# State-space layer of a vision tower: first token as the scan's initial value, product one pair ahead, sums one chunk behind

## The chip, the cores and the metric

One core of a Trainium2 chip. The metric is the device time of one execution in microseconds (us); the kernel is timed in several executions and the median is taken.

## What is computed

A batch of 8 images of 256 x 256 runs through a class-token tower of eight layers on a residual stream of 257 tokens by 256 features: a wavelet tokenizer, memory attention, a mixture of experts, latent attention, a second mixture, **a bidirectional state-space layer**, adapters, a differential attention and a switch layer. The change is in the state-space layer alone. For each of two directions (the second reads the tokens backwards) it computes, with 512 inner features d and 32 states n:

```
u, z   = split(x @ Win.T)
uc     = silu(causal_conv4(u))
dt     = softplus(uc @ Wx_rank @ Wdt + bdt);   B, C = uc @ Wx (32 states each)
h[t,d,n] = exp(dt[t,d] * A[d,n]) * h[t-1,d,n] + dt[t,d] * uc[t,d] * B[t,n],   h before the first token = 0
y[t,d] = sum over n of h[t,d,n] * C[t,n]  + uc * D,  then times silu(z), then @ Wout, a layer norm, and @ Wfuse
```

## The kernel before

Features lie on the 128 partitions and the 257 tokens (T) along the free dimension. The layer is `section_mamba` (L1202). A **unit** is one image in one direction: 16 units, first the 8 forward ones. `units` (L1243) runs them on each engine by a `body` that has the same order of work in each engine's own queue; `before` and `after` say whether a unit has a neighbour whose work is woven into it. The weaving is written by hand as places (n, m).

Within a unit the 512 features are 4 blocks j of 128, and the 32 states are 4 groups q of 8. A **chunk** n = 4j+q (0 to 15, `NCH`) is 8 states of one block, worked as 4 **pairs** m = 0..3 of two states; p = 4n+m numbers the 64 pairs (`SUB`). I call (n, m) a slot. Per pair:

- TensorE, `spread_b` (L1408): two bf16 matmuls that lay one row of B each over all partitions, into a PSUM buffer `pb`. There are 4 rows of `pb`, so two pair buffers; pair p waits for the scans of pair p-2 (semaphore `b_free`).
- VectorE: a product in place (L1740), `pb` times dt*u, for 514 elements, then two scans (L1746) of 257 elements with decays `da` and initial value 0.0, into `hs`. The scans wait for the decays (`da_done`), for the product just before them (`b_set`), and in even m for GpSimd's products of two chunks ago (`hc_done`), since `hs`, `da` and `hc` each have two chunk buffers.
- ScalarE, `decay` (L1617): two exponentials. It works one chunk ahead of VectorE: `decay(n+1, m)` waits until pair (n-1, m) is scanned.
- GpSimd: `hc` = `hs` * C (L1344), four states at a time, two halves per chunk; half 0 waits for scan (n,1) and for the sums of chunk n-2 (`y_free`), half 1 for scan (n,3).
- TensorE, `total` (L1416): adds up the states by fp32 matmuls with the identity, 8 per chunk. In slot (n, m) it issues `spread_b(n, m)` and then `total(n-2, m)`, two chunks behind; in the first two chunks of a unit these are the last two of the unit before.

In chunks 0 to 3 TensorE also spreads the C rows (`spread_c`, L1403, two per slot, behind the sum), ScalarE copies them to SBUF (`cb`, L1648), one pair of copies behind each decay pair, and GpSimd's chunk n waits for its copies (`c_free`).

The next unit's head and the last unit's tail lie in between. On TensorE: projections (L1385) in chunks 4, 5, 7, 8, `b_c_rank` in 9, time steps in 10 to 12; `outward` (L1435) of the unit before in chunk 6, behind a wait for the fourth `take_u` (`proj_free`), then mean, variance, fuse. On ScalarE: `take_u` (L1549, convolution taps of one block, lines L1554 and L1555) behind the decays in chunks 4 to 6, `take_z` (L1557: four silus, a silu of 1028 elements, a table load back) behind chunk 7's, rank, time steps, `soften` and `stack` in 9 to 13; `take_out`, `square`, `root`, `affine` ahead of the decays in 7, 10, 11, 12. On GpSimd: `soften` (L1318, six instructions) behind hc in chunks 0, 2, 12, 14, `taps` (L1304, three of 514 elements) in 5 and 6, small work in 1, 3, 9, 10. On VectorE: `out_chunk` (L1707, two instructions) at (2,0), (6,0), (10,0), (14,0), `center` (L1716) at (9,3), `scale` (L1720) at (11,2), `add` (L1727 or L1729) at (13,2).

`pb` takes four of the eight PSUM banks, `py` (sums) two, `pm` (everything else) two.

Of the kernel before, what the change touches and what calls it, by code (L numbers as in the profile page):

```python
# [17 lines left out]
BF16 = mybir.dt.bfloat16  # L18
# [1183 lines left out]
def section_mamba(nc, k, con, dirs, bfuse):  # L1202
# [6 lines left out]
    with ExitStack() as ctx:  # L1209
# [15 lines left out]
        da = sb("da", [P, 2, NQ_, T])  # L1225
# [43 lines left out]
        with nc.Block() as block:  # L1269
# [19 lines left out]
            def _(pool):  # L1289
# [41 lines left out]
                def body(u, v, d, before, after):  # L1331
                    scanned, summed, c_free = Turn(u, SUB, 2), Turn(u, NCH, 2), Turn(u, NS_, 2)
# [43 lines left out]
            def _(pe):  # L1376
# [31 lines left out]
                def spread_b(u, v, n, m):  # L1408

                    pe.wait_ge(s["b_free"], Turn(u, SUB, 2)(4 * n + m - 1))  # L1410
                    for o in range(2):
                        st = (n % QN) * NQ_ + 2 * m + o
                        ins = nc.tensor.matmul(pb[:, 2 * (m % 2) + o, 0:T], sel[:, st, :], bst2[:, v, :], start=True, stop=True)  # L1413
                    ins.then_inc(s["b_done"], 1)
# [43 lines left out]
                def body(u, v, d, before, after):  # L1458
                    if before is not None:
                        pe.wait_ge(s["f_out"], u + 1)  # L1460
                    pe.wait_ge(s["stacked"], u + 1)
                    pe.wait_ge(s["dt_free"], Turn(u, DJ)(DJ))
                    for n in range(NCH):
                        for m in range(4):
                            spread_b(u, v, n, m)
                            if n >= 2:
                                total(u, n - 2, m)
                            elif before is not None:
                                total(u - 1, NCH - 2 + n, m)
# [3 lines left out]
                            if after is not None:  # L1473
# [64 lines left out]
            def _(act):  # L1538
# [78 lines left out]
                def decay(u, v, d, n, m, free):  # L1617
# [1072 lines left out]
```

## Time and profile before

| what | value |
|---|---|
| time, median of 3 runs | 4842.3 us (4804.22 to 4862.68) |
| the profiled execution | 4836.52 us, its span 4834.8 us |
| TensorE, VectorE, ScalarE, GpSimd busy | 3729.3, 2845.8, 2055.7, 1813.0 us |
| mean granted TensorE clock | 0.895 of 2.4 GHz |

The span runs from the first to the last instruction. Busy time is the union of an engine's instructions, and neighbours overlap a little: an instruction's recorded end lies later than the start of the next, so what an instruction costs its engine is read from start to start in the timeline. The state-space layer lies from about 1571 to 3780 us.

### The profile page before, as it was taken

To read this page: it belongs to the slowest core of one execution; us is meant where nothing else is said; L and a number is where in the kernel's file an instruction comes from. 1 tells how busy PE (TensorE), PEld (TensorE's weight loads), DVE (VectorE), ACT (ScalarE), POOL (GpSimd) and SP (SyncE) were. 2 spreads that over 40 slices of the span, in tenths; PEclk is the share of its full clock that TensorE was granted. 3 is DMA by queue.
4 is the path that set the end of the run, shared out by engine and by line. 5 is a ranking of instruction groups with operands and counts; after the bars stand their busy time and mean duration, and the time that the engine had idled before them with its cause. 6 is when DMAs were issued, how large, how long until landed. Compare 5 with 4: busy or idle time off the path is not lost. (4 is left out here: it accounts for less than half of the span.)

```text
span 4834.8 us, 61153 instructions
## 1 busy us (share of the span) xinstructions
PE 3729.3 (77%) x19350; PEld 2506.0 (52%) x19350; DVE 2845.8 (59%) x4980; ACT 2055.7 (43%) x4651; POOL 1813.0 (37%) x1405
## 2 busy tenths in 40 slices
PE   2848758987986777777778887777776778888857
PEld 1525445655653455555555555555554655555534
DVE  5311224443222999899999999898999433333331
ACT  1211112223113666666666656666665233333322
POOL 0120110000102777777777777777776000000011
PEclk9679959998998899989999999898999999999965
DMA  2157520001472000000000000000000000000035
GB/s 80 45 185 264 210 56 1 1 1 48 163 272 90 1 1 1 2 1 2 1 11 1 1 7 1 2 1 2 1 1 1 9 22 1 1 1 1 1 117 167
DMA packets 94875, 214.46 MB, mean 44 GB/s; under 512 B 13792, under 2 KB 69088, under 8 KB 84224
## 3 DMA queue, kind: packets, MB, share of 16 engines
q1 hardware_dynamic: 71136, 177.89, 10.8%
q0 software_dynamic: 6400, 16.85, 1.1%
q10 hardware_dynamic: 16992, 15.47, 0.9%
q8 instruction: 172, 2.82, 0.2%
q14 instruction: 175, 1.43, 0.1%
HBM read 166.61 MB, written 43.56 MB: 43 GB/s over the span
## 5 line engine op out<-in xcount | busy, mean ns | idle before, releaser
L1344 POOL TENSOR_TENSOR ssm_hc<-ssm_hs,ssm_cb 128x1028 f32<-128x1028 f32 x512 | 1204.5, 2367 | 525.0 <-PE ssm_py L1425 411.9
L1746 DVE TENSOR_TENSOR_SCAN ssm_hs<-ssm_da,ssm_pb 128x257 f32<-128x257 f32 x2048 | 1299.1, 677 | 125.5 <-ACT ssm_da L1625 4.5
L1425 PE MATMUL ssm_py<-ssm_hc,ident 128*128 128x257 f32 x4096 | 1155.2, 407 | 3.5 <-issue 3.5
L1625 ACT ACTIVATE ssm_da<-ssm_dt,ssm_an 128x256 f32<-128x256 f32 x2048 | 878.4, 505 | 155.4 <-DVE ssm_hs L1746 149.6
L1425 PEld LDWEIGHTS ssm_py<-ssm_hc,ident 128*128 128x128 f32 x4096 | 760.5, 207 | 97.2 <-issue 4.1
L1740 DVE TENSOR_TENSOR ssm_pb<-ssm_pb,ssm_dtu 128x514 f32<-128x514 f32 x1024 | 695.0, 679 | 96.6 <-PE ssm_pb L1413 59.2
L1413 PE MATMUL ssm_pb<-ssm_bst,ssm_sel 96*128 96x257 bf16 x2048 | 430.5, 294 | 410.4 <-DVE ssm_hs L1746 400.1
L1413 PEld LDWEIGHTS ssm_pb<-ssm_bst,ssm_sel 96*128 96x128 bf16 x2048 | 143.1, 101 | 732.9 <-DVE ssm_hs L1746 678.7
L1095 DVE TENSOR_REDUCE duo_mxr<-duo_ring 128x4 f32<-128x1024 f32 x128 | 156.6, 1225 | 315.0 <-PE duo_ring L828 303.9
L2182 PE MATMUL moe_pu<-moe_up,moe_xt 128*128 128x512 f32 x568 | 277.4, 612 | 54.4 <-issue 52.5
L1648 ACT COPY ssm_cb<-ln_ps 128x257 f32<-128x257 f32 x512 | 166.1, 377 | 218.7 <-PE ln_ps L1406 217.8
L2079 POOL DMA_INDIRECT moe_yg<-moe_y_dram,moe_slot x51 | 48.2, 945 | 554.5 <-DMA moe_y_dram<-moe_yo 539.5
L2458 DVE COPY moe_ht<-moe_pz 128x512 f32<-128x512 f32 x71 | 49.1, 692 | 298.8 <-PE moe_pz L2192 298.8
L822 PE MATMUL duo_ring<-duo_k,duo_q 32*128 32x256 f32 x1024 | 146.2, 403 | 45.3 <-DVE duo_mxr L1095 45.0
L2182 PEld LDWEIGHTS moe_pu<-moe_up,moe_xt 128*128 128x128 f32 x568 | 100.5, 194 | 145.0 <-issue 140.8
L986 ACT ACTIVATE duo_ex<-duo_ring 128x1024 f32<-128x1024 f32 x128 | 130.9, 1024 | 102.5 <-PE duo_ring L828 102.5
L728 POOL TENSOR_TENSOR duo_qb<-duo_bm,duo_q 128x4 f32<-128x4 f32 x32 | 6.3, 197 | 425.3 <-ACT duo_k L970 425.3
L728 POOL TENSOR_TENSOR lat_qb<-lat_bm,lat_q 128x4 f32<-128x4 f32 x32 | 6.4, 200 | 421.6 <-DVE lat_k L1083 421.6
L822 PEld LDWEIGHTS duo_ring<-duo_k,duo_q 32*128 32x128 f32 x1024 | 93.4, 187 | 101.3 <-issue 47.5
L828 PE MATMUL duo_ring<-duo_q,duo_k 32*128 32x256 f32 x1024 | 145.9, 404 | 0.0
L1385 PE MATMUL ln_ps<-xb,ssm_win 128*128 128x257 f32 x512 | 135.4, 388 | 12.1 <-ACT ssm_e L1555 6.5
L282 PE MATMUL ln_ps<-h,mean 128*128 128x257 f32 x160 | 55.8, 481 | 112.0 <-PEq L80 62.0
(528 smaller groups left out, 5941.1 us busy)
## 6 DMA issues: line engine op xcount, KB each, us to landing
moe_up<-in_moe_up SPq DMA_DIRECT2D x72, 1024.0 KB, 5.0
moe_down<-in_moe_down SPq DMA_DIRECT2D x72, 512.0 KB, 5.8
moe_xr<-moe_x_dram SPq DMA_DIRECT2D x71, 128.0 KB, 5.7
moe_y_dram<-moe_yo ACTq DMA_DIRECT2D x71, 128.0 KB, 1.7
sw_wt<-in_sw_w SPq DMA_DIRECT2D x47, 192.5 KB, 2.5
sw_x_dram<-sw_zero SPq DMA_DIRECT2D x1, 6016.0 KB, 19.4
sw_xr<-sw_x_dram SPq DMA_DIRECT2D x47, 128.0 KB, 2.4
sw_y_dram<-sw_yo ACTq DMA_DIRECT2D x47, 128.0 KB, 1.7
```

The lines of the kernel that those rows point to most:

```text
L822: ins1 = nc.tensor.matmul(dst1[:, o, at:at + w], q[r, b1, t * P:t * P + P], kk[r, b1, a, 0:w], start=not causal, stop=not causal or t == 1)
L828: ins2 = nc.tensor.matmul(dst2[:, o, at:at + 256 - q0], kk[r, b2, a, t * P:t * P + P], q[r, b2, q0:256], start=not causal, stop=not causal ...
L1095: ins = nc.vector.tensor_reduce(mxr[:, a, js, :], src.rearrange("p o (t s) -> p o t s", t=2), AX, ALU.max)
L1344: nc.gpsimd.tensor_tensor(hc[:, n % 2, part_], hs[:, n % 2, part_], cb[:, q * NQ_ + 4 * half:q * NQ_ + 4 * half + 4, :], ALU.mult).then_in ...
L1385: ins = nc.tensor.matmul(pm[:, n % 2, 0:T], w_in[:, c, n * P:n * P + P], k.xb[:, c, 0:T], start=(c == 0), stop=(c == C - 1))
L1413: ins = nc.tensor.matmul(pb[:, 2 * (m % 2) + o, 0:T], sel[:, st, :], bst2[:, v, :], start=True, stop=True)
L1425: ins = nc.tensor.matmul(py[:, j % 2, 0:T], k.ident[:], hc[:, n % 2, st, :], start=(q == 0 and st == 0), stop=(q == QN - 1 and st == NQ_ - 1))
L1625: ins = nc.scalar.activation(da[:, n % 2, 2 * m + o, 1:T], dt2[:, v, j, 1:T], ACT.Exp, scale=a_n[:, d, j, st:st + 1])
L1648: nc.scalar.copy(cb[:, st, :], pm[:, st % 2, 0:T]).then_inc(s["c_free"], 1)
L1740: nc.vector.tensor_tensor(b2, b2, dtu2[:, v, j:j + 1, :].broadcast_to([P, 2, T]), ALU.mult).then_inc(s["b_set"], 1)
L1746: ins = nc.vector.tensor_tensor_scan(hs[:, n % 2, 2 * m + o, :], da[:, n % 2, 2 * m + o, :], b2[:, o, :], 0.0, ALU.mult, ALU.add)
L2182: ins = nc.tensor.matmul(pu[:, b % 2, g, :], xt[:, b % 2, c, :], up[:, b % WR, c, g * HID:g * HID + HID], start=(c == 0), stop=(c == C - 1))
```

## The change

- `pb` becomes four pair buffers of 2 x 256 elements (a pair in one bank); token 0 is taken out of it. B's first token comes by its own small matmul (`first_b`), ScalarE copies it to `b0` (`take_first`), and once per chunk ScalarE writes dt*u*B of token 0 for the chunk's 8 states into `hs[..., 0]` (`start`). Scans take that as initial value and run over tokens 1 to 256.
- VectorE issues the product of pair p+1 ahead of the scans of pair p; TensorE spreads B two pairs ahead of the slot and may do so when the scans of four pairs ago are done.
- TensorE sums chunk n-1 in chunk n.
- The fourth `take_u` moves ahead of the decays in chunk 6.

Core of the diff (semaphore names, the memset of `da` that goes, and the copy of the identity to bf16 for `first_b` left out):

```diff
-        da = sb("da", [P, 2, NQ_, T])
+        eyeb = sb("eyeb", [3 * NS_, NS_], BF16)
+        b0 = sb("b0", [P, 2, NS_])
+        da = sb("da", [P, 2, NQ_, T - 1])
-        pb = ps("pb", [P, 4, BANK])
+        pb = ps("pb", [P, 4, 2, T - 1])
...
+                def first_b(u, v):
+                    pe.wait_ge(s["stacked"], u + 1)
+                    nc.tensor.matmul(pm[:, 0, 0:NS_], bst2[:, v, 0:1].broadcast_to([3 * NS_, P]), eyeb[:], start=True, stop=True).then_inc(s["first_done"], 1)
-                def spread_b(u, v, n, m):
-                    pe.wait_ge(s["b_free"], Turn(u, SUB, 2)(4 * n + m - 1))
+                def spread_b(u, v, p):
+                    pe.wait_ge(s["b_free"], Turn(u, SUB, 4)(p - 3))
                     for o in range(2):
-                        ins = nc.tensor.matmul(pb[:, 2 * (m % 2) + o, 0:T], sel[:, st, :], bst2[:, v, :], start=True, stop=True)
+                        ins = nc.tensor.matmul(pb[:, p % 4, o, :], sel[:, st, :], bst2[:, v, 1:T], start=True, stop=True)
...
-                    pe.wait_ge(s["stacked"], u + 1)
+                    pe.wait_ge(s["first_out"], u + 1)
                     for n in range(NCH):
                         for m in range(4):
-                            spread_b(u, v, n, m)
-                            if n >= 2:
-                                total(u, n - 2, m)
+                            if 4 * n + m + 2 < SUB:
+                                spread_b(u, v, 4 * n + m + 2)
+                            elif after is not None:
+                                spread_b(u + 1, 1 - v, 4 * n + m + 2 - SUB)
+                            if n:
+                                total(u, n - 1, m)
                             elif before is not None:
-                                total(u - 1, NCH - 2 + n, m)
+                                total(u - 1, NCH - 1, m)
...
+                                if (n, m) == (14, 2):
+                                    if before is not None:
+                                        pe.wait_ge(s["f_out"], u + 2)
+                                    first_b(u + 1, 1 - v)
...
+                def take_first(u, v):
+                    act.wait_ge(s["first_done"], u + 1)
+                    nc.scalar.copy(b0[:, v, :], pm[:, 0, 0:NS_]).then_inc(s["first_out"], 1)
+
+                def start(u, v, n, free):
+                    j, q = n // QN, n % QN
+                    if n == 0:
+                        act.wait_ge(s["first_out"], u + 1)
+                    if free is not None:
+                        act.wait_ge(s["hc_done"], free)
+                    nc.scalar.activation(hs[:, n % 2, :, 0], b0[:, v, q * NQ_:q * NQ_ + NQ_], ACT.Copy, scale=dtu2[:, v, j, 0:1]).then_inc(s["h_first"], 1)
...
                     for n in range(NCH):
+                        if n == 6 and after is not None:
+                            take_u(u + 1, 1 - v, after, 3)
...
+                        free = Turn(u, 2 * NCH, 4)(2 * n) if n or before is not None else None
+                        if n + 1 < NCH:
+                            start(u, v, n + 1, free)
+                        elif after is not None:
+                            start(u + 1, 1 - v, 0, free)
...
-                            if n == 6:
-                                take_u(u + 1, 1 - v, after, 3)
...
+                            if n == 14:
+                                take_first(u + 1, 1 - v)
...
+                def product(u, v, p):
+                    j = p // (4 * QN)
+                    if p % (4 * QN) == 0:
+                        dve.wait_ge(s["dt_set"], Turn(u, DJ)(j + 1))
+                    b2 = pb[:, p % 4]
+                    dve.wait_ge(s["b_done"], Turn(u, SUB)(p + 1))
+                    nc.vector.tensor_tensor(b2, b2, dtu2[:, v, j:j + 1, 1:T].broadcast_to([P, 2, T - 1]), ALU.mult).then_inc(s["b_set"], 1)
...
                         for m in range(4):
-                            b2 = pb[:, 2 * (m % 2):2 * (m % 2) + 2, 0:T]
-                            dve.wait_ge(s["b_done"], Turn(u, SUB)(4 * n + m + 1))
-                            nc.vector.tensor_tensor(b2, b2, dtu2[:, v, j:j + 1, :].broadcast_to([P, 2, T]), ALU.mult).then_inc(s["b_set"], 1)
+                            p = 4 * n + m
+                            if p + 1 < SUB:
+                                product(u, v, p + 1)
+                            elif after is not None:
+                                product(u + 1, 1 - v, 0)
                             if m % 2 == 0:
                                 dve.wait_ge(s["hc_done"], Turn(u, 2 * NCH, 4)(2 * n + m // 2 - 3))
+                            if m == 0:
+                                dve.wait_ge(s["h_first"], Turn(u, NCH)(n + 1))
+                            dve.wait_ge(s["da_done"], Turn(u, SUB)(p + 1))
+                            dve.wait_ge(s["b_set"], Turn(u, SUB)(p + 1))
                             for o in range(2):
-                                ins = nc.vector.tensor_tensor_scan(hs[:, n % 2, 2 * m + o, :], da[:, n % 2, 2 * m + o, :], b2[:, o, :], 0.0, ALU.mult, ALU.add)
+                                st = 2 * m + o
+                                ins = nc.vector.tensor_tensor_scan(hs[:, n % 2, st, 1:T], da[:, n % 2, st, :], pb[:, p % 4, o, :], hs[:, n % 2, st, 0:1], ALU.mult, ALU.add)
```

## Rows read from the trace of the kernel before

**Rows 1.** Stretches view: length; busy PE, PEld, DVE, ACT, POOL; clock. Layer, one unit.

```profile
1577.00:3760.00 2183.00, 1714.03 (x7835) 1182.42 (x7836) 1989.23 (x3254) 1355.77 (x3288) 1620.38 (x1067) 0.92 0.01 2
...
2582.00:2718.60 136.60, 108.58 (x497) 75.16 (x497) 124.61 (x205) 86.27 (x209) 102.49 (x69) 0.92 0.00 1
```

**Rows 2.** The page's list of costliest groups, three of the layer.

```profile
L1344 POOL TENSOR_TENSOR ssm_hc<-ssm_hs,ssm_cb 128x1028 f32<-128x1028 f32 x512 | 1204.5, 2367 | 525.0 <-PE ssm_py L1425 411.9
L1746 DVE TENSOR_TENSOR_SCAN ssm_hs<-ssm_da,ssm_pb 128x257 f32<-128x257 f32 x2048 | 1299.1, 677 | 125.5 <-ACT ssm_da L1625 4.5
...
L1740 DVE TENSOR_TENSOR ssm_pb<-ssm_pb,ssm_dtu 128x514 f32<-128x514 f32 x1024 | 695.0, 679 | 96.6 <-PE ssm_pb L1413 59.2
```

**Rows 3.** Timeline of VectorE: start, duration, line, idle before it.

```profile
2614.37 0.68 DVE L1740 TENSOR_TENSOR ssm_pb<-ssm_pb,ssm_dtu 128x514 f32<-128x514 f32 x1
2615.15 1.27 DVE L1746 TENSOR_TENSOR_SCAN ssm_hs<-ssm_da,ssm_pb 128x257 f32<-128x257 f32 x2
2616.33 0.67 DVE L1716 TENSOR_TENSOR ln_cen<-ln_sq,ln_ps 128x514 f32<-128x514 f32 x1
2616.91 0.70 DVE L1740 TENSOR_TENSOR ssm_pb<-ssm_pb,ssm_dtu 128x514 f32<-128x514 f32 x1
...
2618.92 0.47 DVE L1710 SCALAR_TENSOR_TENSOR ssm_py<-ssm_uc,ssm_cols,ssm_py 128x257 f32<-128x257 f32 x1
2619.42 0.42 DVE L1712 TENSOR_TENSOR ssm_zs<-ssm_zs,ssm_py 128x257 f32<-128x257 f32 x1
2619.76 0.69 DVE L1740 TENSOR_TENSOR ssm_pb<-ssm_pb,ssm_dtu 128x514 f32<-128x514 f32 x1
...
2648.08 0.85 DVE L1727 SCALAR_TENSOR_TENSOR h<-ln_ps,ssm_lnc,h 128x257 f32<-128x257 f32 x2
2648.85 0.69 DVE L1740 TENSOR_TENSOR ssm_pb<-ssm_pb,ssm_dtu 128x514 f32<-128x514 f32 x1
```

**Rows 4.** Who waited for whom over the execution: us, times, longest.

```profile
DVE ssm_pb L1740 <- PE ssm_pb L1413: 59.2, 40, 2.6
```

**Rows 5.** Timeline of TensorE and VectorE in chunk 6 of a unit.

```profile
2718.50 2.08 PE L1435 MATMUL ln_ps<-ssm_zs,ssm_wout 128*128 128x257 f32 x4 [3.18 <-ACT ssm_e L1555]
...
2721.05 0.70 DVE L1740 TENSOR_TENSOR ssm_pb<-ssm_pb,ssm_dtu 128x514 f32<-128x514 f32 x1 [2.25 <-PE ssm_pb L1413]
```

**Rows 6.** Timeline of ScalarE: two copies of C rows; silu, table load, decays.

```profile
2667.18 0.65 ACT L1648 COPY ssm_cb<-ln_ps 128x257 f32<-128x257 f32 x2 [4.56 <-PE ln_ps L1406]
...
2739.30 1.05 ACT L1562 ACTIVATE ssm_uc<-ssm_e 128x1028 f32<-128x1028 f32 x1
2740.37 1.28 ACT L1563 ACT_TABLE_LOAD   x1
2741.67 3.70 ACT L1625 ACTIVATE ssm_da<-ssm_dt,ssm_an 128x256 f32<-128x256 f32 x9
```

**Rows 7.** Timeline of TensorE at the high and at the low clock.

```profile
2665.79 0.38 PE L1413 MATMUL ssm_pb<-ssm_bst,ssm_sel 96*128 96x257 bf16 x2 [0.82 <-DVE ssm_hs L1746]
2666.01 1.03 PE L1425 MATMUL ssm_py<-ssm_hc,ident 128*128 128x257 f32 x4
2666.88 0.38 PE L1406 MATMUL ln_ps<-ssm_cst,ssm_sel 96*128 96x257 bf16 x2
...
2690.64 1.92 PE L1425 MATMUL ssm_py<-ssm_hc,ident 128*128 128x257 f32 x4
2692.35 0.64 PE L1406 MATMUL ln_ps<-ssm_cst,ssm_sel 96*128 96x257 bf16 x2
```

**Rows 8.** Timeline of GpSimd: soften begins, hc behind it; taps, hc behind them.

```profile
2678.41 0.72 POOL L1323 TENSOR_TENSOR ssm_e<-ssm_e,ssm_dtu 128x257 f32<-128x257 f32 x1
...
2683.38 4.69 POOL L1344 TENSOR_TENSOR ssm_hc<-ssm_hs,ssm_cb 128x1028 f32<-128x1028 f32 x2
...
2732.45 1.28 POOL L1310 TENSOR_TENSOR ssm_e<-ssm_e 128x514 f32<-128x514 f32 x1
...
2736.50 2.36 POOL L1344 TENSOR_TENSOR ssm_hc<-ssm_hs,ssm_cb 128x1028 f32<-128x1028 f32 x1
```

More of the change, by code:

```diff
@@ L1331, in body @@
                 def body(u, v, d, before, after):
-                    scanned, summed, c_free = Turn(u, SUB, 2), Turn(u, NCH, 2), Turn(u, NS_, 2)
+                    scanned, summed, c_free = Turn(u, SUB, 4), Turn(u, NCH, 2), Turn(u, NS_, 2)
                     for n in range(NCH):
@@ L1523, in _ @@
                     time_step(0, j)
+                first_b(0, 0)
+                for p in range(2):
+                    spread_b(0, 0, p)
                 units(pe, body)
                 last = UN - 1
-                for n in (NCH - 2, NCH - 1):
-                    for m in range(4):
-                        total(last, n, m)
+                for m in range(4):
+                    total(last, NCH - 1, m)
                 pe.wait_ge(s["f_out"], last + 2)
@@ L1638, in body @@
                         for m in range(4):
-                            free = Turn(u, SUB, 2)(4 * (n - 1) + m + 1) if n or before is not None else None
+                            free = Turn(u, SUB, 4)(4 * (n - 1) + m + 1) if n or before is not None else None
                             if n + 1 < NCH:
@@ L1681, in _ @@
                 stack(0, 0)
+                take_first(0, 0)
                 for m in range(4):
                     decay(0, 0, 0, 0, m, None)
+                start(0, 0, 0, None)
                 units(act, body)
@@ L1695, in _ @@
                 link = Link(dve, k.dve_link)
-                link(nc.vector.memset(da[:, :, :, 0:1], 0.0))
                 dve.wait_ge(s["w_in"], 16 * 13)
                 nc.vector.tensor_scalar_min(a_n[:], a_n[:], 83.0).then_inc(s["rates"], 1)
+                nc.vector.tensor_copy(eyeb[:], eye3[:])
                 nc.vector.tensor_copy(sel[:], eye3[:].unsqueeze(2).broadcast_to([3 * NS_, NS_, P])).then_inc(s["sel_set"], 1)
-                dve.sem_inc(s["b_free"], 2)
+                dve.sem_inc(s["b_free"], 4)
                 dve.sem_inc(s["y_free"], 2)
@@ L1733, in body @@
                     for n in range(NCH):
-                        j, q = n // QN, n % QN
-                        if q == 0:
-                            dve.wait_ge(s["dt_set"], Turn(u, DJ)(j + 1))
+                        q = n % QN
+                        j = n // QN
                         for m in range(4):
-                            b2 = pb[:, 2 * (m % 2):2 * (m % 2) + 2, 0:T]
-                            dve.wait_ge(s["b_done"], Turn(u, SUB)(4 * n + m + 1))
-                            nc.vector.tensor_tensor(b2, b2, dtu2[:, v, j:j + 1, :].broadcast_to([P, 2, T]), ALU.mult).then_inc(s["b_set"], 1)
+                            p = 4 * n + m
[3 more added lines that the diff above has]
+                                product(u + 1, 1 - v, 0)
@@ L1741, in body @@
                             if m % 2 == 0:
                                 dve.wait_ge(s["hc_done"], Turn(u, 2 * NCH, 4)(2 * n + m // 2 - 3))
-                            dve.wait_ge(s["da_done"], Turn(u, SUB)(4 * n + m + 1))
-                            dve.wait_ge(s["b_set"], Turn(u, SUB)(4 * n + m + 1))
+                            if m == 0:
+                                dve.wait_ge(s["h_first"], Turn(u, NCH)(n + 1))
+                            dve.wait_ge(s["da_done"], Turn(u, SUB)(p + 1))
@@ L1758, in body @@
                                     add(u - 1, before)
+                product(0, 0, 0)
                 units(dve, body)
```

6 lines of the change are left out of this document (3 added, 3 removed).

## The prediction

> **What bounds the kernel now.** The change lies in one of nine stages, the state-space layer, so I first cut that stage out with the stretches view. From 1577 to 3760 us VectorE is busy 1989 of 2183 us, GpSimd 1620, TensorE 1714 and ScalarE 1356 [rows 1]: VectorE sets the pace. The layer is sixteen units (8 images, two directions); one of them is the stretch of 136.6 us. A unit has 64 slots (n,m), n = 0..15, m = 0..3, and a slot on VectorE is a product (L1740) and two scans (L1746). I call the end of the last scan of chunk n F(n).
>
> The cost list gives what VectorE spends on the two [rows 2]: 1299 us in 2048 scans with 125.5 us idle in front of them, which the view gives almost nobody as releaser, and 695 us in 1024 products. 125.5/1024 = 0.12 us a slot is the scan's wait for the product just before it (semaphore b_set). The timeline shows it better, from start to start [rows 3]: a product holds VectorE 0.78 us when its own scan follows (2614.37 to 2615.15; 0.80 in even slots), but an instruction of the same 514 elements holds it 0.58 when the follower depends on nothing recent (L1716 at 2616.33, product at 2616.91). Two scans take 1.18. So a slot is 1.97 to 1.99, 64 make 126.7, and the rest of VectorE's unit is four pairs L1710/L1712 at 0.84, L1716 and L1720 at 0.58, and 0.77 for the two of L1727: 5.3. With some 4 us of true waiting this is 136.6.
>
> That waiting is TensorE's late B rows: 59.2 us in 40 waits [rows 4]. It sits in chunk 6: TensorE waits 3.18 us for the last convolution copy of ScalarE (L1555) before it may start L1435, and VectorE then lacks the input of a product for 2.25 us [rows 5] and that of the next for somewhat less.
>
> **The parts of the change, with prices.**
> *Product one pair ahead, four pair buffers.* Between product p+1 and its scan there now lie two scans, so the product costs 0.58 and not 0.79: -0.21 us a slot. One token fewer (256 for 257, 512 for 514) is worth under 0.01. This asks that B rows come two slots earlier, which the buffers permit: TensorE may write pair p once scan p-4 is done.
>
> The 0.78 with a wait and the 0.58 without stand in the timeline [rows 3]. The Trainium skill speaks against this term: its page "VectorE: DVE Perf Modes", section "The DRAIN you can't avoid", says that the next VectorE op does not start until the pipe has emptied and that a semaphore between two ops "costs nothing extra here". By that rule the term would be 0; the trace does not agree, and I go by the trace.
>
> *First token as initial value.* 2048 scans read their start from memory and not from the instruction. No scan here does. The nearest rows: L1712 (two tensors, 257 elements) holds VectorE 0.34 us (2619.42 to 2619.76), L1727, which also reads a per-partition value, (2648.85-2648.08)/2 = 0.385 [rows 3]. Bounds 0 and 0.045 us a scan (0 to 92 us in all); I take 0.045, the only row of that kind. A slot becomes 0.58+1.18+0.09 = 1.86 (bounds 1.77 and 1.86). Four slots: 7.44. VectorE's unit: 64 x 1.86 + 5.3 = 124.3.
>
> *take_u of the fourth block ahead of the decays of chunk 7.* It no longer waits for scan (5,3), so the wait of chunk 6 goes. I give it 52 of the 59.2 us (the rest is start-up and single late rows), 3.7 us in each of the 14 units that have both neighbours.
>
> *ScalarE's new work*: 16 starts of 128x8 and one copy per unit, 0.2 to 0.3 us each by my estimate (two copies of 257 elements take 0.65 in [rows 6]): 4 to 5 us in a unit where ScalarE has 50 free. The work costs nothing, but its place does: start(n+1) stands behind all four decays and, in chunks 0 to 3, behind the eight copies of C of chunk n, and scan (n+1,0) waits for it. Before, that scan needed the first decay only. It also waits for GpSimd's products of chunk n-1, both halves.
>
> *Sums one chunk behind.* GpSimd's 412 us of waits for TensorE [rows 2] go, and TensorE gets a wait instead: in slot (n,0) it waits for half 0 of hc(n-1), in (n,2) for half 1, and behind it in its queue stand C rows, projections and the B rows of the next slots. I follow that through a unit. Durations: B or C pair 0.22, total pair 0.87, another fp32 pair 0.87 [rows 7]; two halves of hc 4.7, one 2.35, soften 4.97, taps 4.05 [rows 8]; the last of two copies ends 0.95 behind its C pair (2666.88 to 2667.83), more when a decay runs; silu of 1028 elements 1.05, table load 1.28, a decay 0.41 [rows 6].
>
> Clock from F(14)=0, F(15)=7.4. GpSimd: hc(14) to 2.4, soften to 7.4, hc(15) to 9.8 and 12.1. TensorE (0,0) is held to 9.8, then a slot costs 0.87+0.22+0.22 = 1.31; C rows 6, 7 go out at 14.6, copied 15.65, start(1) 15.9; VectorE wants it at 15.5: late 0.45, and 0.35 by product 7. hc(0) begins at 15.65 (it needs those copies), half 0 to 18.0; the same again: start(2) at 24.2, wanted 23.4: 0.8. hc(0) ends 20.4, soften 25.3, half 0 of hc(1) 27.7; TensorE is held to that, B rows for product 11 come 0.9 late, start(3) 0.4 late. Chunk 3: 0.65. hc(2) runs from 33.6 to 38.3, soften to 43.2, half 0 of hc(3) to 45.6; TensorE (4,0) then does total, projection and the B rows: ready 47.7, wanted 45.1: 2.55. Together 6.1 us.
>
> Clock from F(5)=0 (F(6)=8.3, F(7)=15.7, F(8)=23.4): hc(5) to 2.45, taps to 6.5, hc(6) to 11.2, taps to 15.25, half 0 of hc(7) to 17.6. TensorE (8,0): total, projection, B rows, total, projection to 21.3. ScalarE: silu 21.8, silu 1028 22.9, table load 24.15, four decays 27.4, start(9) 27.7. VectorE wants it at 24.0: 3.7 late; with 0.2 for product 35, 3.9. In chunks 9 to 15 I find every answer in time, by 1.3 us or more.
>
> *Sum.* Unit: 136.6 - 64x0.12 (7.7) - 3.7 + 6.1 + 3.9 = 135.2; walking VectorE's own clock round (124.3 + 9.8, where late answers overlap and the small old waits fall away) gives 134.1. I take the walk: -2.5 x 14 = -35. First and last unit have half of the stalls: -6. A start-up copy and wait: +1. TensorE's clock: in the unit the mean grant is 0.92 [rows 1], that is 0.08/0.5 or 0.16 of the time (22 us) at 1.2 GHz and not 2.4, and a total pair then costs 1.71 instead of 0.87 [rows 7]. Until now such stretches had cover; where TensorE is held by GpSimd it has none. I put 1 us a unit on it, +14. Sum -26. The profiled execution took 4836.5 us (span 4834.8), 6 below the median of the runs, 4842.3: 4836.5-26 = 4810.
>
> **The rivals.**
> 1. *The new waits are hidden* (against the walk; for it: GpSimd is busy 102 of 136 us and could be earlier than I think). Then -7.7-3.7 in 14 units, -7.7 in two: -175, 4661. With a free initial value another -92: 4570.
> 2. *The initial value costs nothing.* Only 30 to 35 slots of a unit are not tied to the GpSimd-TensorE loop, so -2.8 us a unit, not -5.8: 4765.
> 3. *Slower: a loop takes over.* Place: chunks 0 to 4 and 8. C rows wait behind the sum, the sum for GpSimd, GpSimd for the copies of the C rows. With TensorE at 1.2 GHz a slot is near 2.6 and the loop 2.35+4x2.6 = 12.7 against 7.44. If half of the 22 us a unit falls there, half of those 11 us is lost: 5 us, unit 139.2 and not 134.1, 4836.5+14x2.6 = 4873. It decides from 2.5 us of added waits a unit. For it: TensorE will stand still 2 to 3 us at (8,0), and before the low stretch of chunk 6 it stood still 3.18 us [rows 5].
> 4. *No overlap of product and scan.* A product still holds VectorE 0.79 with other scans behind it: slot 1.97+0.09 = 2.06, +5.8 a unit, -3.7, and some 5 of the 10 us of stalls (they shrink when VectorE is slower): +7 x 15 = +105, 4940. Against it are the 0.58 us [rows 3]; this is also the case in which the change does not do what it says. (It is what the Trainium skill's section named above would have.)
>
> **How the numbers follow.** Forecast 0.47; rival 1 0.17 (in part or in full); rival 2 0.15; rival 3 0.18; rival 4 0.03. The measurement tells about 2% from no change, so faster means under 4745, slower over 4939. Faster: rival 1 (0.15), half of rival 2 (0.06), the low tail of the forecast (0.06): 0.27. Slower: rival 4 (0.02), the upper end of rival 3 (0.06), others 0.02: 0.10. Range: up to rival 3 with its spread, 4895, down to the price of rival 1, 4665. The forecast's own range is 4765 to 4860.
>
> **What the profile after would show.** Product to next scan start 0.58 and no 0.12 us in front of each scan. Scans of 0.72 us if the initial value costs, 0.67 if not. No wait of L1435 for L1555 in chunk 6. GpSimd's wait for TensorE's sums nearly gone; in its place TensorE waits for hc, above all in slots (4,0), (7,0) and (8,0). Scans with a wait for ScalarE's start in chunks 1 to 4, and one of 3 to 4 us at (9,0). Unit near 134 us. The prediction is wrong if TensorE's waits for hc are there and VectorE has none, or if VectorE waits over 12 us a unit.

## The result and the profile after

The changed kernel takes 4919.6 us (median of 4 runs, 4918.3 to 4948.6) against 4839.6 (4804.2 to 4862.7): a ratio of 1.0186, interval 1.0113 to 1.0259 (here and in the table below the ratio is the record's estimate over all runs, not the quotient of the two medians). I had forecast 4810 with a range of 4665 to 4895. The profiled execution took 4919.25 us, its span is 4917.5.

The stretches view of the changed kernel: the layer, then two stretches of 5 us.

```profile
1577.00:3850.00 2273.00, 1758.28 (x7833) 1258.55 (x7834) 2017.88 (x3243) 1403.65 (x3571) 1619.11 (x1072) 0.89 0.01 2
2720.00:2725.00 5.00, 1.39 (x3) 1.17 (x4) 4.98 (x8) 0.00 (x0) 4.92 (x4) 0.82 0.00 0
2725.00:2730.00 5.00, 5.00 (x17) 3.54 (x16) 2.82 (x5) 2.90 (x8) 0.87 (x1) 0.50 0.02 3
```

The layer answers to [rows 1]: 90 us longer, TensorE's granted clock 0.89 and not 0.92, and VectorE idle for 255 us of it where it was idle for 194. From the first scan to the end of the last the layer now lasts 2276 us (before: 2184). That length is my measure below, since what lies outside the layer differs by up to 61 us from one profiled execution to another (2608 us in e5, 2669 in f3), in parts of the program that no kernel here alters.

The cost list of the changed kernel, four of the layer's largest groups (L1797 is the scan, L1777 the product, L1346 GpSimd's hc, L1432 the sum):

```profile
L1432 PE MATMUL ssm_py<-ssm_hc,ident 128*128 128x257 f32 x4096 | 1230.1, 427 | 385.0 <-POOL ssm_hc L1346 384.8
L1797 DVE TENSOR_TENSOR_SCAN ssm_hs<-ssm_da,ssm_hs,ssm_pb 128x256 f32<-128x256 f32 x2048 | 1410.5, 731 | 103.0 <-ACT ssm_hs L1655 93.0
L1346 POOL TENSOR_TENSOR ssm_hc<-ssm_hs,ssm_cb 128x1028 f32<-128x1028 f32 x512 | 1204.0, 2363 | 619.2 <-DVE ssm_hs L1797 410.6
...
L1777 DVE TENSOR_TENSOR ssm_pb<-ssm_pb,ssm_dtu 128x512 f32<-128x512 f32 x1024 | 697.6, 681 | 178.9 <-PE ssm_pb L1420 144.1
```

Held against [rows 2]: GpSimd no longer waits for TensorE's sums (411.9 us before). TensorE instead stands 385 us in front of its sums, waiting for GpSimd. VectorE's 0.12 us in front of every scan is gone; the 103 us there now are the late start (L1655), and its products wait 144 us for B rows, where they waited 59.2 [rows 4]. A scan, recorded, has grown from 677 to 731 ns.

VectorE's timeline away from the stalls, which answers to [rows 3]:

```profile
2603.98 0.68 DVE L1777 TENSOR_TENSOR ssm_pb<-ssm_pb,ssm_dtu 128x512 f32<-128x512 f32 x1
2604.57 1.38 DVE L1797 TENSOR_TENSOR_SCAN ssm_hs<-ssm_da,ssm_hs,ssm_pb 128x256 f32<-128x256 f32 x2
2605.86 0.68 DVE L1777 TENSOR_TENSOR ssm_pb<-ssm_pb,ssm_dtu 128x512 f32<-128x512 f32 x1
```

A product holds VectorE 0.59 us from start to start, two scans 1.29: a slot of 1.875 us. I forecast 1.86.

I took the start of every scan pair out of VectorE's timeline and subtracted the undisturbed slot and the known insertions (L1748 and the like) from each distance; what is left over is lost waiting. Mean of the 14 units with both neighbours:

| | slot | unit | lost a unit | where |
|---|---|---|---|---|
| before | 1.985 | 137.2 | 4.9 | chunk 6: 3.7 |
| after | 1.875 | 143.3 | 18.0 | chunks 0 to 4: 3.2, 2.6, 1.9, 2.7, 2.3 (12.7); around (9,0): 5.1 |

A wait in front of the first scan of chunk n+1 is counted to chunk n here. So the places are those of the prediction but for chunk 0, to which the walk gave 0.45 us and not 3.2, and the wait of chunk 6 is gone. The size is not the predicted one: 18 us where the walk had 10. What a stall looks like, in the timeline of TensorE (first chunk of a unit, and the first sum of chunk 2):

```profile
2717.77 1.03 PE L1432 MATMUL ssm_py<-ssm_hc,ident 128*128 128x257 f32 x4
...
2723.61 2.08 PE L1432 MATMUL ssm_py<-ssm_hc,ident 128*128 128x257 f32 x4 [3.73 <-POOL ssm_hc L1346]
2725.49 0.64 PE L1408 MATMUL ln_ps<-ssm_cst,ssm_sel 96*128 96x257 bf16 x2
2725.92 0.63 PE L1420 MATMUL ssm_pb<-ssm_bst,ssm_sel 96*128 96x256 bf16 x2
2726.34 1.92 PE L1432 MATMUL ssm_py<-ssm_hc,ident 128*128 128x257 f32 x4
...
2735.12 1.14 PE L1432 MATMUL ssm_py<-ssm_hc,ident 128*128 128x257 f32 x4 [2.87 <-POOL ssm_hc L1346]
...
2744.71 2.08 PE L1432 MATMUL ssm_py<-ssm_hc,ident 128*128 128x257 f32 x4 [4.07 <-POOL ssm_hc L1346]
```

and of VectorE and GpSimd in the same chunks:

```profile
2726.59 0.70 DVE L1777 TENSOR_TENSOR ssm_pb<-ssm_pb,ssm_dtu 128x512 f32<-128x512 f32 x1 [1.61 <-PE ssm_pb L1420]
...
2732.70 4.68 POOL L1346 TENSOR_TENSOR ssm_hc<-ssm_hs,ssm_cb 128x1028 f32<-128x1028 f32 x2 [6.83 <-ACT ssm_cb L1679]
```

TensorE stands 3.73 us for GpSimd, and the sum behind it takes 2.08 us where the one before took 1.03. In the 5 us from 2725 the granted clock is 0.50, the lower of its two levels (1.2 GHz). A slot of TensorE then lasts 2.7 us (2723.61 to 2726.34), 1.3 at the upper level (2736.09 to 2737.41). The C rows come out later by that, ScalarE's copies behind them, GpSimd's hc of this chunk behind those (6.83 us of waiting), and that sets the next sum. Behind 4.07 us the same happens; behind 2.87 the sum takes 1.14 and the clock holds.

Around chunk 8 a stand of 2.33 us precedes slower projections (L1387: 1.58 us, then 1.15, where 1.03 is usual), the silus wait for them, and the start of chunk 9 comes 3.44 us late:

```profile
2653.61 1.14 PE L1432 MATMUL ssm_py<-ssm_hc,ident 128*128 128x257 f32 x4 [2.33 <-POOL ssm_hc L1346]
2654.59 1.58 PE L1387 MATMUL ln_ps<-xb,ssm_win 128*128 128x257 f32 x4
...
2665.52 1.39 DVE L1797 TENSOR_TENSOR_SCAN ssm_hs<-ssm_da,ssm_hs,ssm_pb 128x256 f32<-128x256 f32 x2 [3.44 <-ACT ssm_hs L1655]
```

### The profile page after: what moved, and what is told of

Same layout as the page of the kernel before. It is cut to its first block and busy times, and to the rows that moved or that the text cites. A ratio compares the mean times of both kernels' runs of the same rounds, so it can differ in the third digit from the quotient of the medians.

```text
span 4917.5 us, 61727 instructions
## 1 busy us (share of the span) xinstructions
PE 3749.6 (76%) x19366; PEld 2567.9 (52%) x19366; DVE 2881.8 (59%) x4980; ACT 2098.2 (43%) x4923; POOL 1812.7 (37%) x1405
## 5 line engine op out<-in xcount | busy, mean ns | idle before, releaser
L1432 PE MATMUL ssm_py<-ssm_hc,ident 128*128 128x257 f32 x4096 | 1230.1, 427 | 385.0 <-POOL ssm_hc L1346 384.8
L1797 DVE TENSOR_TENSOR_SCAN ssm_hs<-ssm_da,ssm_hs,ssm_pb 128x256 f32<-128x256 f32 x2048 | 1410.5, 731 | 103.0 <-ACT ssm_hs L1655 93.0
L1346 POOL TENSOR_TENSOR ssm_hc<-ssm_hs,ssm_cb 128x1028 f32<-128x1028 f32 x512 | 1204.0, 2363 | 619.2 <-DVE ssm_hs L1797 410.6
L1432 PEld LDWEIGHTS ssm_py<-ssm_hc,ident 128*128 128x128 f32 x4096 | 788.8, 214 | 551.4 <-POOL ssm_hc L1346 431.6
L1777 DVE TENSOR_TENSOR ssm_pb<-ssm_pb,ssm_dtu 128x512 f32<-128x512 f32 x1024 | 697.6, 681 | 178.9 <-PE ssm_pb L1420 144.1
L1420 PE MATMUL ssm_pb<-ssm_bst,ssm_sel 96*128 96x256 bf16 x2048 | 433.1, 296 | 119.6 <-DVE ssm_hs L1797 115.0
L1420 PEld LDWEIGHTS ssm_pb<-ssm_bst,ssm_sel 96*128 96x128 bf16 x2048 | 190.2, 105 | 333.7 <-DVE ssm_hs L1797 219.5
L1387 PE MATMUL ln_ps<-xb,ssm_win 128*128 128x257 f32 x512 | 149.2, 419 | 8.2 <-DVE ssm_sel L1738 4.8
```

Source lines behind the costliest of these rows:

```text
L1346: nc.gpsimd.tensor_tensor(hc[:, n % 2, part_], hs[:, n % 2, part_], cb[:, q * NQ_ + 4 * half:q * NQ_ + 4 * half + 4, :], ALU.mult).then_in ...
L1387: ins = nc.tensor.matmul(pm[:, n % 2, 0:T], w_in[:, c, n * P:n * P + P], k.xb[:, c, 0:T], start=(c == 0), stop=(c == C - 1))
L1420: ins = nc.tensor.matmul(pb[:, p % 4, o, :], sel[:, st, :], bst2[:, v, 1:T], start=True, stop=True)
L1432: ins = nc.tensor.matmul(py[:, j % 2, 0:T], k.ident[:], hc[:, n % 2, st, :], start=(q == 0 and st == 0), stop=(q == QN - 1 and st == NQ_ - 1))
L1777: nc.vector.tensor_tensor(b2, b2, dtu2[:, v, j:j + 1, 1:T].broadcast_to([P, 2, T - 1]), ALU.mult).then_inc(s["b_set"], 1)
L1797: ins = nc.vector.tensor_tensor_scan(hs[:, n % 2, st, 1:T], da[:, n % 2, st, :], pb[:, p % 4, o, :], hs[:, n % 2, st, 0:1], ALU.mult, ALU.add)
```

## The experiments

"Layer" is from the first scan to the end of the last in the profiled execution; slot, unit and lost are the tally above. Ratios are to the kernel before, run on the same chip.

| run | median us | ratio (interval) | layer | slot | unit | lost |
|---|---|---|---|---|---|---|
| before | 4839.6 | | 2184 | 1.985 | 137.2 | 4.9 |
| after | 4919.6 | 1.0186 (1.0113 to 1.0259) | 2276 | 1.875 | 143.3 | 18.0 |
| e1 sums two behind | 4664.4 | 0.9623 (0.9583 to 0.9662) | 2024 | 1.875 | 126.8 | 1.5 |
| e2 C rows first | 4909.2 | 1.0144 (1.0100 to 1.0188) | 2264 | 1.875 | 142.8 | 17.5 |
| e3 start early | 4917.9 | 1.0142 (1.0094 to 1.0189) | 2273 | 1.875 | 143.1 | 17.8 |
| e4 zero initial value | 4863.5 | 1.0032 (1.0005 to 1.0058) | 2221 | 1.755 | 139.8 | 22.2 |
| e5 keep the clock | 4859.0 | 1.0064 (1.0030 to 1.0099) | 2214 | 1.875 | 139.2 | 13.9 |
| e6 take_u alone | 4759.7 | 0.9853 (0.9786 to 0.9919) | 2132 | 1.985 | 133.5 | 1.2 |
| e7 two behind, start early | 4813.0 | 0.9948 (0.9913 to 0.9983) | 2153 | 1.875 | 135.3 | 10.0 |
| e8 product between scans | 4665.5 | 0.9643 (0.9555 to 0.9731) | 2032 | 1.78 | 127.5 | 8.3 |
| f1 one behind alone | 5093.5 | 1.0553 (1.0530 to 1.0576) | 2434 | 1.985 | 153.5 | 21.1 |
| f2 two behind, take_u back | 4758.1 | 0.9830 (0.9778 to 0.9881) | 2122 | 1.875 | 133.9 | 8.6 |
| f3 two behind, own slot | 4902.9 | 1.0157 (1.0129 to 1.0185) | 2237 | 2.09 | 140.1 | 1.0 |

The experiments ran on three chips: the kernel before had a median of 4839.6 us beside e1 to e4, 4838.1 beside e5 to e8 and 4829.2 beside f1 to f3. Where runs of different chips are compared below, the difference of their medians can be off by some 10 us, and the layer's length is the better measure.

**e1. The changed kernel with the sums two chunks behind again.**

```diff
-                            if n:
-                                total(u, n - 1, m)
+                            if n >= 2:
+                                total(u, n - 2, m)
                             elif before is not None:
-                                total(u - 1, NCH - 1, m)
+                                total(u - 1, NCH - 2 + n, m)
```

> The changed kernel with one part undone: TensorE sums chunk n-2 in chunk n again; everything else of the change stays. Theory A (the loop: with sums one chunk behind TensorE waits for GpSimd's hc, and the B and C rows queued behind the sum come late, at a clock that the standing still has lowered): the unit falls from 143.3 us by most of the 12.5 us that VectorE loses in chunks 0 to 4 and by about 3 in chunk 8, to 128 to 131 us; time 4710 to 4760; TensorE's wait for hc (385 us) gone, GpSimd's wait for TensorE's sums back (some 200 to 400 us) and harmless. Theory B (the place of ScalarE's start behind the decays and copies is the price, 93 us of waits): 4830 to 4919. Theory C (the initial value read from memory is the price, 0.055 us a scan): unchanged, 4919.

4664 us, 255 below the changed kernel and 175 below the kernel before, and 46 below what theory A allowed at best; theories B and C are out as the main cause. The cost list of e1 from 1577 us on:

```profile
L1798 DVE TENSOR_TENSOR_SCAN ssm_hs<-ssm_da,ssm_hs,ssm_pb 128x256 f32<-128x256 f32 x2039 | 1401.4, 729 | 14.7 <-ACT ssm_hs L1656 11.8 <-POOL ssm_hc L1346 2.6 <-issue 0.3
L1346 POOL TENSOR_TENSOR ssm_hc<-ssm_hs,ssm_cb 128x1028 f32<-128x1028 f32 x511 | 1200.8, 2367 | 365.7 <-PE ssm_py L1432 300.7 <-ACT ssm_cb L1680 36.8 <-DVE ssm_hs L1798 22.5
L1432 PE MATMUL ssm_py<-ssm_hc,ident 128*128 128x257 f32 x4096 | 1092.4, 390 | 1.2 <-POOL ssm_hc L1346 1.2
...
L1778 DVE TENSOR_TENSOR ssm_pb<-ssm_pb,ssm_dtu 128x512 f32<-128x512 f32 x1018 | 686.8, 675 | 2.0 <-issue 1.2 <-PE ssm_pb L1420 0.5
```

TensorE's 385 us of waiting for hc are 1.2, and everything that VectorE waited for goes with them. GpSimd waits 301 us for TensorE again, which costs nothing here: 1.5 us a unit are lost. The sums' place makes 16.5 of the 18.0 us a unit. Putting it back also makes the wait for the start nearly vanish (93 to 12 us), though the start's own place is unchanged.

**f1. The other side: the kernel before, with the sums one chunk behind and nothing else** (the same edit the other way round).

> The kernel before with one edit: TensorE sums chunk n-1 in chunk n. No initial value, no product ahead, no moved convolution, no start. Theory (the place of the sums is what costs, whoever waits behind it): the wait of TensorE for GpSimd's products of chunk n-1 stands ahead of the B rows of the next slot, and here B rows are only one slot ahead of VectorE, not two. The sum's place cost 18.0 - 1.5 = 16.5 us a unit in the changed kernel; I expect 12 to 18 here, about +230 us: 5070 (4980 to 5130), with VectorE's products waiting for TensorE's B rows for over 150 us. Rival (the price belongs to the pair of one-behind sums and the late start of the initial value, which the kernel before has not): only the C-row loop is left, 2 to 4 us a unit, 4870 to 4900.

5093.5, 264 above the kernel before, near the theory's 5070. VectorE's products wait for B rows:

```profile
DVE ssm_pb L1739 <- PE ssm_pb L1413: 291.3, 208, 3.5
```

The edit costs 250 us of layer in this kernel, which has no start of an initial value, and 252 in the changed one, which has it. The rival is out, and the other parts hide none of it.

**e2 and e3. Which wait, if not the sums' place?** e2 issues the C rows of a slot ahead of its sum; e3 issues the start behind the second pair of decays and not behind the fourth and the copies.

```diff
+                            if n < QN:
+                                spread_c(u, v, NQ_ * n + 2 * m)
+                                spread_c(u, v, NQ_ * n + 2 * m + 1)
                             if n:
                                 total(u, n - 1, m)
...
                             if n < QN:
-                                spread_c(u, v, NQ_ * n + 2 * m)
-                                spread_c(u, v, NQ_ * n + 2 * m + 1)
```

> The changed kernel, but in chunks 0 to 3 TensorE issues the two C rows of a slot ahead of the sum and not behind it. A: cuts the link sum -> C rows -> copies -> hc and start, so chunks 0 to 3 lose 6 to 8 us less a unit and hc(3) is earlier for slot (4,0); B rows of chunk 4 and 8 stay late: 4810 to 4850. B: start(n+1) no longer waits for late copies in chunks 1 to 4, but for the rest: 4860. C: 4919.

> The changed kernel, but ScalarE's start of the next chunk stands behind the second decay pair and not behind all four and their copies. A: only the wait at (9,0) shrinks (1.6 of 3.4 us), chunks 1 to 4 stay tied to late B rows: 4880 to 4905. B: the 93 us of waits for start go nearly all: 4830. C: 4919.

Neither moves the time: their medians lie 10 and 2 us below the changed kernel's, and the runs of all three overlap. The numbers of A and B both missed, and C's 4919 was met without C being right: its cause, the initial value, is not the price (e1, e4). What moved is the name of the wait. Who waited for whom, first e2, then e3 (us in total, times, longest):

```profile
DVE ssm_pb L1777 <- PE ssm_pb L1420: 180.1, 137, 4.5
...
DVE ssm_hs L1797 <- ACT ssm_hs L1655: 58.0, 36, 3.4
```

```profile
DVE ssm_pb L1778 <- PE ssm_pb L1420: 208.6, 146, 4.7
...
DVE ssm_hs L1798 <- ACT ssm_hs L1655: 28.7, 16, 2.3
```

The wait for the start falls from 93 to 58 and 29, the one for B rows rises from 144 to 180 and 209. I read both as answers of one late loop, where the sooner of them only uncovers the other. Something else moved too: over the four executions of each the mean granted clock is 0.873 in e2 and 0.876 in e3, in the changed kernel 0.885. So some of what the edits gave may have gone into a lower clock; no run separates the two.

**e4. Initial value 0.0 in every scan** (the contribution of each unit's first token is left out; everything else, the start too, is still issued).

```diff
-ins = nc.vector.tensor_tensor_scan(hs[:, n % 2, st, 1:T], da[:, n % 2, st, :], pb[:, p % 4, o, :], hs[:, n % 2, st, 0:1], ALU.mult, ALU.add)
+ins = nc.vector.tensor_tensor_scan(hs[:, n % 2, st, 1:T], da[:, n % 2, st, :], pb[:, p % 4, o, :], 0.0, ALU.mult, ALU.add)
```

> The changed kernel, but the scans take the constant 0.0 as initial value (the first token's contribution is left out of the states; start still writes it). The scan should return from 0.645 to 0.59 us start to start, the slot from 1.875 to 1.765. C: all 2048 x 0.055 = 113 us come back: 4806. A: only the slots that are not tied to the loop (30 to 40 of 64) give anything: 45 to 65 us, 4855 to 4875, and the other slots show the same wait longer.

```profile
L1797 DVE TENSOR_TENSOR_SCAN ssm_hs<-ssm_da,ssm_pb 128x256 f32<-128x256 f32 x2048 | 1284.0, 668 | 104.1 <-ACT ssm_hs L1655 91.4 <-issue 12.8
```

A scan takes 668 ns, not 731, and the slot is 1.755, 0.01 less than expected: the initial value costs 0.06 us a scan from start to start (0.053 net against the scans of 257 elements before: two took 1.186 us, now 1.293). Of the 7.7 us a unit that this frees (64 x 0.12) the unit gets 3.5, and the waits grow from 18.0 to 22.2. More than half of the gain is lost to the loop, as A said.

**e5. Eight matmuls that nobody reads, ahead of the sums in six slots of a unit**, to keep TensorE at work where it would stand.

```diff
+                            if (n, m) in ((0, 0), (1, 0), (2, 0), (3, 0), (4, 0), (8, 0)) and (n or before is not None):
+                                pe.wait_ge(s["b_free"], Turn(u, SUB, 4)(4 * n))
+                                for _ in range(8):
+                                    nc.tensor.matmul(pb[:, (4 * n + 3) % 4, 0, 0:P], k.ident[:], k.ident[:], start=True, stop=True)
                             if n:
                                 total(u, n - 1, m)
```

> The changed kernel with eight added matmuls of the identity (128 columns, result overwritten by the next B rows) in slots (0,0), (1,0), (2,0), (3,0), (4,0), (8,0), where TensorE otherwise stands still for GpSimd's hc. They do no useful work; they wait for what the next B rows wait for. Theory K (a good part of the stalls is TensorE at 1.2 GHz just behind each standing still): VectorE's loss in chunks 0 to 4 falls from 12.7 us a unit to 7 to 9, granted clock in the layer up from 0.89 to 0.94 or more, time 4830 to 4870. Theory L (the order of the waits alone makes the loss): no gain, the added work costs 0 to 1 us a unit, 4919 to 4935.

4859 us, 61 below the changed kernel; the layer is 62 shorter. TensorE's timeline at two such places and at one without added matmuls:

```profile
2683.61 2.05 PE L1479 MATMUL ssm_pb<-ident 128*128 128x128 f32 x16
2687.70 1.14 PE L1432 MATMUL ssm_py<-ssm_hc,ident 128*128 128x257 f32 x4 [2.04 <-POOL ssm_hc L1346]
...
2701.68 2.05 PE L1479 MATMUL ssm_pb<-ident 128*128 128x128 f32 x16
2705.77 1.42 PE L1432 MATMUL ssm_py<-ssm_hc,ident 128*128 128x257 f32 x4 [2.03 <-POOL ssm_hc L1346]
...
2790.14 2.08 PE L1432 MATMUL ssm_py<-ssm_hc,ident 128*128 128x257 f32 x4 [3.82 <-POOL ssm_hc L1346]
```

and the stretches view of chunks 0 to 4 of one unit, in the changed kernel, e5 and e1:

```profile
2721.70:2772.60 50.90, 36.30 (x162) 27.31 (x163) 39.64 (x64) 29.99 (x86) 35.07 (x28) 0.83 0.00 1
2667.70:2713.70 46.00, 39.85 (x240) 32.20 (x239) 39.28 (x63) 29.81 (x87) 35.07 (x28) 0.96 0.00 1
2582.00:2620.50 38.50, 30.51 (x161) 20.90 (x160) 38.47 (x64) 28.35 (x80) 36.14 (x29) 1.00 0.01 1
```

Work that computes nothing, put into a queue that is too late already, makes the kernel faster: chunks 0 to 4 lose 8.3 us a unit, not 12.7, chunk 8 loses 4.3, not 5.1, and the layer's granted clock is 0.93, not 0.90 (theory K had 0.94 or more). The added matmuls can only delay TensorE's queue, so the gain is the clock's. In the 14 middle units, chunks 0 to 4 have 19.2 us a unit at the lower level in the changed kernel and 3.9 in e5. They do not hold the clock everywhere: at 2705.77 it falls even so, and the last row of TensorE's timeline shows a place without them. So the clock is a part of the loss, at least 4 us a unit; 13.9 are left, and e5 loses 1.2 of them in chunk 11, where the changed kernel loses nothing.

**e6. The kernel before with the fourth take_u ahead of the decays of chunk 6, alone.**

```diff
+                        if n == 6 and after is not None:
+                            take_u(u + 1, 1 - v, after, 3)
                         if n == 7 and before is not None:
...
-                            if n == 6:
-                                take_u(u + 1, 1 - v, after, 3)
```

> The kernel before with one part of the change alone: the fourth take_u ahead of the decays of chunk 6. If its price is what the prediction says, the 3.7 us that VectorE loses in chunk 6 go in 14 units: 4785 to 4795. If another wait takes its place (the decays of chunk 7 come 1.5 us later), 4820 to 4840.

```profile
L1740 DVE TENSOR_TENSOR ssm_pb<-ssm_pb,ssm_dtu 128x514 f32<-128x514 f32 x1022 | 693.5, 679 | 16.5 <-PE ssm_pb L1413 10.4 <-issue 6.0
```

The unit is 3.7 us shorter, the layer 52, which is the predicted price to the digit. The stand of 3.18 us in chunk 6 [rows 5] goes with it, and the layer's granted clock is 0.96 where it was 0.92. The median falls by 78, more than expected; the other 26 lie outside the layer of the profiled execution, and no part of the edit reaches there. The interval (down 0.8 to 2.1%) holds both numbers.

**f2. e1 with that take_u back in its old place.**

> The changed kernel with sums two chunks behind, as in e1, and the fourth take_u back behind the decays of chunk 6. Theory (its price is the late B rows of chunk 6, as alone): +3.7 us in 14 units, 4664 + 52 = 4716, up to 4664 + 78 = 4742 if it is worth what it was alone. Rival (with four pair buffers TensorE is a slot further ahead and covers half of it): +1.8 a unit, 4690.

94 us above e1 (on another chip; the layer is 98 longer), more than either theory had. TensorE and VectorE in chunk 6 of f2:

```profile
2672.99 2.08 PE L1442 MATMUL ln_ps<-ssm_zs,ssm_wout 128*128 128x257 f32 x4 [5.67 <-ACT ssm_e L1572]
...
2675.53 0.70 DVE L1778 TENSOR_TENSOR ssm_pb<-ssm_pb,ssm_dtu 128x512 f32<-128x512 f32 x1 [4.03 <-PE ssm_pb L1420]
```

In [rows 5] these are 3.18 and 2.25. The same wait is longer, I take it because VectorE now gets to chunk 6 sooner and ScalarE's convolution does not; 5.9 us a unit are lost in chunk 6 and 2.3 in chunk 8. TensorE's stand reaches VectorE less 1.64 us (5.67 to 4.03), where it was 0.93 (3.18 to 2.25): the extra buffers cover far from half, so the rival is wrong, and so is the theory's price, which took the wait as a constant.

**f3. e1 with product p in its own slot.**

```diff
-                            if p + 1 < SUB:
-                                product(u, v, p + 1)
-                            elif after is not None:
-                                product(u + 1, 1 - v, 0)
+                            product(u, v, p)
```

> The changed kernel with sums two chunks behind, as in e1, and product p in its own slot right before its scans, not one pair ahead. Theory (a product that is waited for by its next neighbour costs 0.21 more, and the initial value 0.055 a scan): slot 1.875 + 0.21 = 2.085, a unit 126.8 + 13.4 = 140.2, 16 units +215: 4880. Rival by which a product holds VectorE no shorter when it is ahead (what e1 gained came from elsewhere): 4665 to 4700.

```profile
2604.40 0.68 DVE L1778 TENSOR_TENSOR ssm_pb<-ssm_pb,ssm_dtu 128x512 f32<-128x512 f32 x1
2605.18 1.38 DVE L1795 TENSOR_TENSOR_SCAN ssm_hs<-ssm_da,ssm_hs,ssm_pb 128x256 f32<-128x256 f32 x2
```

4903 us, 238 above e1 (on another chip) and 23 above the expected 4880; the layer is 213 longer, where the sum was 215. The same instruction of the same size holds VectorE 0.78 us (0.80 in even slots) when the next one waits for it and 0.58 to 0.59 when two scans lie between.

**e8. The gain without the buffers.** The kernel before, take_u moved, and product p+1 issued between the two scans of pair p. Two pair buffers do for that; there is no initial value and no start.

```diff
                             for o in range(2):
                                 ins = nc.vector.tensor_tensor_scan(hs[:, n % 2, 2 * m + o, :], da[:, n % 2, 2 * m + o, :], pb[:, 2 * (p % 2) + o, 0:T], 0.0, ALU.mult, ALU.add)
+                                if o == 0:
+                                    if p + 1 < SUB:
+                                        product(u, v, p + 1)
+                                    elif after is not None:
+                                        product(u + 1, 1 - v, 0)
```

> The kernel before with take_u moved and one other edit: VectorE issues the product of pair p+1 between the two scans of pair p. No further buffers, no initial value from memory, no start, sums two behind. If what the change gains is only that product and scan no longer stand side by side, a slot falls from 1.985 to 1.77 us: 64 x 0.21 = 13.6 us a unit, less what TensorE's B rows cost with only two pair buffers (they may start when the scans of p-1 are done and have 0.6 us): with 2 to 4 us a unit lost there 4610 to 4650. If B rows are late in every slot (by 0.2 us or more), 4730 to 4790.

VectorE's timeline of e8:

```profile
2603.01 1.26 DVE L1750 TENSOR_TENSOR_SCAN ssm_hs<-ssm_da,ssm_pb 128x257 f32<-128x257 f32 x2
2604.19 0.69 DVE L1738 TENSOR_TENSOR ssm_pb<-ssm_pb,ssm_dtu 128x514 f32<-128x514 f32 x1
2604.78 1.26 DVE L1750 TENSOR_TENSOR_SCAN ssm_hs<-ssm_da,ssm_pb 128x257 f32<-128x257 f32 x2
```

4665.5, as e1 within the noise, though above the expected 4610 to 4650. One scan between product and reader is enough: the slot is 1.78. The price is that B rows must come within about one scan (0.6 us) of the scans that free their buffer. VectorE's products wait 76 us for them and 8.3 us a unit are lost, 6.8 more than in e1, about what the cheaper scans save (0.095 x 64 = 6.1).

**e7. e1 with the start behind the second decay pair**, to take e1's last waits.

> As the run with sums two behind (4664 us), and start behind the second decay pair. What VectorE still loses there is 1.5 us a unit, 0.9 of it in chunk 8. If that is start's place: 4645 to 4658. If start now blocks ScalarE (it waits for GpSimd with two decay pairs behind it): 4670 to 4700.

4813, 149 above e1 (on another chip; the layer is 129 longer) and over 110 above what either theory expected; the direction is that of the second. Who waited for whom:

```profile
ACT ssm_hs L1656 <- POOL ssm_hc L1346: 474.8, 164, 5.2
```

The start needs GpSimd's products of the chunk whose buffer it writes, both halves. Ahead of two decay pairs and the copies it holds all of ScalarE's queue until these are done. With the sums two behind GpSimd is late by design; of the two places tried, only the one at the end of ScalarE's chunk hides that.

## Why the prediction was wrong

**The step that failed** is the size of the stalls of "Sums one chunk behind": 6.1 us a unit in chunks 0 to 4 was 12.7, 3.9 around (9,0) was 5.1, and the 1 us a unit for TensorE's clock was far too little. Unit: 134.1 plus 1 predicted, 143.3 measured. The 8.2 between them are 1.0 of slot (1.875 for 1.86) and 7.2 of waits (18.0 for 10.8). Measured against before, a middle unit grew by 6.1 us where the sum had -2.5 and +1, so by 7.6 more than forecast (the sum started from one unit of 136.6 us; the mean of the middle ones is 137.2); 14 x 7.6 = 106 us of the 109 by which the profiled execution passed 4810. The prediction's own sign of being wrong, over 12 us of waits a unit, is there.

Why it was too small: I walked the loop sum, C rows, copies, hc, sum at the upper clock throughout, and spread a mean of the clock over the unit. But the clock was low behind stands of TensorE such as those of 3.73 and 4.07 us above, and the change puts these stands at the head of the loop: the mean grant in chunks 0 to 4 of a unit is 0.83. A case of it stood in my own rows: 3.18 us of standing in chunk 6 [rows 5] with 2.08 us behind it. I used it for rival 3 and not for the sum. In chunks 0 to 4 the walk was 6.6 us short (12.7 for 6.1); in e5, where 3.9 us a unit are left there at the lower clock, 2.2 of that remain (8.3). So about 4.4 are the clock. How the 2.2 divide between the low stretches that are left, the cost of the added matmuls and errors of a hand walk (it had 0.45 for chunk 0, where 3.2 are lost, 1.3 in e5) is open.

**Rival 3 is nearest to what happened**, and slower than its 4873: its places, the slot of 2.6 us at the low clock (2.7 measured) and about the size of its loss by the clock (5 us a unit; e5 shows 4) are as written, and it was past its point (2.5 us of added waits) by far. Its loop through the C rows is not shown to be the one that binds: e2 cuts it and gains nothing clear of noise. Its chance, 0.18, was low for a case that needed only 2.5 us a unit more than the forecast's own 10.

**Product one pair ahead**: right, from 0.78 or 0.80 to 0.58 a product; 213 us of layer in f3. The Trainium skill's "VectorE: DVE Perf Modes", section "The DRAIN you can't avoid", has a semaphore after each of eight copies cost no more than one after the last. f3 against e1 is not that experiment but the case where the next instruction needs the product, and there the wait costs 0.21 us a product (213 us in 1024); the trace does not agree with the rule that the prediction drew from it. The same section also says that a next op that is not held starts earlier, which the prediction left out. Rival 4 is out.

**Initial value**: taken 0.045, was 0.06 a scan in e4, 0.053 net of the one element less. Rival 2 is out.

**take_u**: right, 3.7 us a unit alone (e6). It is worth 98 us of layer once VectorE is faster (f2 against e1), so it is no constant.

**Rival 1** (waits hidden, 4661) is false for the change as made. With the sums two behind the waits are hidden and the time is 4664; that the number fits so well is partly luck, since the layer fell by 160 us and not by the rival's 175.

**The accounts.** The runs form a chain from before to after, in us of layer: take_u -52 (before to e6), initial value with its start and the four buffers +105 (e6 to f3), product ahead -213 (f3 to e1), sums one behind +252 (e1 to after): 2184 to 2276. The steps add up by construction. Only the second can be held against a sum: 0.053 us in 2048 scans would be 109, and 105 were measured, so start and buffers cost nothing that shows.

## What to carry to other kernels

Before a consumer is moved closer behind its producer, ask what stands behind the consumer in its engine's queue. A wait in an in-order queue is paid by everything behind it, so a lag that looks like waste (GpSimd's 412 us of idle time) can be what keeps the bound engine fed. When a loop is walked, walk it at the clock that TensorE has after the stand which the change creates. The wait for a dependent result went as soon as one other instruction lay between it and its reader (e8); that needs no more buffers if one can be found in the order.

## What was not expected of the hardware

- A stand of 3.73, 3.82, 4.07 or 5.67 us left the four matmuls behind it at 2.08 us, the lower clock; one of 2.87 left them at 1.14. The length of the stand alone does not decide it: in the profiled execution of f1, 29 of 40 stands of 2.5 to 3 us have four matmuls at the lower clock behind them, and 44 of 67 stands of 3 to 3.5 us have them at the upper. Matmuls without a reader, 2 us of them in six places, gave 61 us back.
- A per-partition initial value in memory lengthens a scan over 256 elements from 668 to 731 ns, whether or not anything waits.
- One scan between a product and its reader hides the dependence nearly as well as two do: a slot of e8 has three instructions in 1.78 us, 0.59 each, and none waits for its neighbour.
